# A deeper attention pipeline, with every fourth high half cast on DVE

## The reference

```
x = x + tanh(g_xattn[0]) * xattn(layernorm(x), ctx_2048, ...)     # x, ctx: 8 batches x 256 x 512

q = X @ Wq.T + bq        # 32 heads of 16
k = ctx @ Wk.T + bk      # 8 groups of 16, each group serves 4 heads
v = ctx @ Wv.T + bv
scores = q . k / sqrt(16), masked (a 256 x 256 mask, and a key mask for each batch)
w = softmax(scores)
out = (w @ v) @ Wo.T + bo
```

## Time and profile before

| | us |
|---|---|
| median of 3 runs (1936.1 to 1944.45) | 1940.29 |
| the profiled execution | 1944.32 |
| its span, from the first to the last instruction | 1942.6 |
| busy in the span: PE, PE weight load | 1652.5, 848.3 |
| busy in the span: DVE, ACT, POOL | 975.0, 711.3, 821.8 |

### The profile page before, as it was taken

The page is one execution under the profiler, slowest core; times in us unless marked ns, Lnnn a source line. Parts: engine busy times, 40 slices in busy tenths (PEclk is TensorE's granted clock), DMA queues, the critical chain, the costliest instruction groups (busy, mean ns, idle before and its releaser), DMA issues. The chain is left out here.

```text
span 1942.6 us, 29847 instructions
## 1 busy us (share of the span) xinstructions
PE 1652.5 (85%) x11034; PEld 848.3 (44%) x11034; DVE 975.0 (50%) x1975; ACT 711.3 (37%) x1311; POOL 821.8 (42%) x853
## 2 busy tenths in 40 slices
PE   5589888877874788887799996999999999888897
PEld 3255545544542333433356653444444444343343
DVE  5465556556543577775166563346754333211136
ACT  2176667665674354544122231121111111122221
POOL 1376667666564344444144333423443342011124
PEclk9899999989986899999799997999999999999999
DMA  3531223123141444533346532735654554366655
GB/s 124 144 89 40 72 67 86 41 62 77 29 96 26 85 101 100 98 75 69 66 82 124 103 81 70 159 80 108 125 127 90 124 115 98 76 154 152 153 143 169
DMA packets 423990, 188.36 MB, mean 97 GB/s; under 512 B 365788, under 2 KB 388318, under 8 KB 423848
## 3 DMA queue, kind: packets, MB, share of 16 engines
q1 hardware_dynamic: 418168, 167.85, 38.4%
q0 software_dynamic: 5680, 18.62, 3.8%
HBM read 77.17 MB, written 22.81 MB: 51 GB/s over the span
## 5 line engine op out<-in xcount | busy, mean ns | idle before, releaser
L941 POOL TENSOR_TENSOR a_pl<-a_prob,a_ph 128x512 f16<-128x512 f32 x256 | 294.7, 1162 | 194.3 <-ACT a_prob L862 192.3
L861 ACT ACTIVATE a_ph<-bank 128x512 f16<-128x512 f32 x256 | 153.7, 600 | 148.9 <-PE bank L635 141.2
L1024 DVE TENSOR_REDUCE a_mx<-bank 128x2 f32<-128x512 f32 x256 | 165.4, 684 | 74.8 <-PE bank L617 72.3
L137 PE MATMUL bank<-XTh,d_whs 128*128 128x512 f16 x512 | 195.9, 383 | 0.9 <-ACT e_y L2295 0.7
L138 PE MATMUL bank<-XTl,d_whs 128*128 128x512 f16 x512 | 196.0, 383 | 0.0
L139 PE MATMUL bank<-XTh,d_wls 128*128 128x512 f16 x512 | 195.8, 382 | 0.0
L2133 POOL CAST d_cut<-d_raw 128x512 f16<-128x512 f32 x90 | 57.0, 634 | 239.7 <-DMA d_raw<-in_L_ffn_sw 156.2
L862 ACT ACTIVATE a_prob<-bank 128x512 f32<-128x512 f32 x256 | 154.2, 602 | 0.0
L2053 DVE TENSOR_TENSOR d_hid<-d_hid,bank 128x512 f32<-128x512 f32 x64 | 43.9, 686 | 181.5 <-PE bank L139 181.3
L1266 PE MATMUL bank<-b_wfc,b_xTh 128*128 128x512 f16 x256 | 99.5, 389 | 33.4 <-DMA b_xTl<-f_cut 25.4
L1276 PE MATMUL bank<-b_wpj,b_hTh 128*128 128x512 f16 x256 | 104.7, 409 | 21.9 <-DMA b_hTl<-b_hcut 21.8
(11 more groups left out here) (330 smaller groups left out, 4026.9 us busy)
## 6 DMA issues: line engine op xcount, KB each, us to landing
d_raw<-in_L_ffn_w SPq DMA_DIRECT2D x48, 256.0 KB, 3.1
d_raw<-in_L_ffn_sw SPq DMA_DIRECT2D x42, 256.0 KB, 3.1
made<-e_y SPq DMA_DIRECT2D x39, 256.0 KB, 2.2
a_stage<-in_L_ffn_w_fc SPq DMA_DIRECT2D x32, 256.0 KB, 2.9
a_stage<-in_L_ffn_w_proj SPq DMA_DIRECT2D x32, 256.0 KB, 3.0
a_fbuf<-in_ctx SPq DMA_DIRECT2D x16, 256.0 KB, 3.1
rows<-f_cut SPq DMA_DIRECT2D x16, 256.0 KB, 2.5
out_x<-X SPq DMA_DIRECT2D x16, 256.0 KB, 2.5
```

The costliest lines, as they stand in the source:

```text
L137: nc.tensor.matmul(out_ap, lhi, rhi, start=first, stop=False)
L861: nc.scalar.activation(ph[:, n % NP, :], bank[BST + n % 2][:, :], ACT.Exp)
L941: nc.gpsimd.tensor_tensor(pl[:, n % NP, :], prob[:, n % 2, :], ph[:, n % NP, :], ALU.subtract).then_inc(ev["L"], 1)
L1024: nc.vector.tensor_reduce(mx[:, tt, half, 2 * g:2 * g + 2], bank[BS + m % 2][:, :].rearrange("p (r k) -> p r k", r=2), AX_X, ALU.max)\
```

## The change

Preparation is spread over two batches. In the loop of batch b, q and k, v of batch b+2 are projected (steps 10 to 16) and the first 16 heads of them turned (steps 19 to 22); the other 16 heads of batch b+1 are turned at steps 0 to 3; one plain score and one maximum of batch b+1 stand in every step. The maxima come in halves by heads rather than by queries: those of the first 16 heads leave at step 18, those of the other 16 at step 4 of their own batch, and the turned scores wait for each half only where they begin to use it (steps 0 and 16). `times_v` runs through the end of a batch, the output projection moves to steps 5, 7 and 8, v has three buffers, and the input is loaded one batch earlier. The prologue projects batch 1 as well, inside the plain scores of batch 0, and cuts the input of batch 2.

In steps 2, 6, 10, ... 30 (`CASTS`) ACT takes only the float32 exponential, and DVE makes `ph` by a cast of `prob` from float32 to float16. POOL waits for that cast.

The diff, cut to its core:

```diff
-    vv = sb("a_v", [P, 2, 2, G0, VW], F16)
+    vv = sb("a_v", [P, 3, 2, G0, VW], F16)
...
-    PQ, PK = (0, 3), (1, 4)
-    TQ, TK = (6, 8), (7, 9)
-    FIRST, LAST = 10, 29
+    PQ, PK = (10, 14), (12, 16)
+    TURN0, TURN1 = 19, 0
+    NEG0, NEG1 = 18, 4
+    OTURN, OUT = 5, (7, 8)
+    CASTS = tuple(range(2, 32, 4))
     NORM = LAG + 8
-    OTURN, OUT = 11, (13, 14)
...
-    SUM_AT = [15, 17, 19, 21, 23, 25, 27, 29]
-    CUT_AT = [15, 18, 20, 22, 26, 29]
+    SUM_AT = [1, 5, 9, 13, 17, 21, 25, 29]
+    CUT_AT = [1, 6, 11, 17, 23, 28]
...
@@ PE, turned_scores @@
                 wait("E", b, n + 1, NS)
+                if n % 16 == 0:
+                    wait(f"ng{n // 16}", b, 32, 32)
...
@@ PE, the loop of a batch @@
-                wait("ng", b, 64, 64)
...
-                for n in range(NS + LAG):
-                    if n < NS:
-                        turned_scores(b, par, n)
+                for n in range(NS):
...
+                    turned_scores(b, par, n)
                     if n >= LAG:
-                        times_v(b, par, n - LAG)
+                        times_v(b, n - LAG)
+                    elif b:
+                        times_v(b - 1, NS + n - LAG)
+                    if more:
+                        scores(b + 1, 1 - par, n)
...
                         if n == PQ[tt]:
-                            q_of(nx, tt)
+                            q_of(b + 2, tt)
...
-                    for m in due(n - 1):
-                        scores(nx, 1 - par, m)
...
@@ ACT @@
-                    nc.scalar.activation(ph[:, n % NP, :], bank[BST + n % 2][:, :], ACT.Exp)
+                    if n not in CASTS:
+                        nc.scalar.activation(ph[:, n % NP, :], bank[BST + n % 2][:, :], ACT.Exp)
                     nc.scalar.activation(prob[:, n % 2, :], bank[BST + n % 2][:, :], ACT.Exp).then_inc(ev["E"], 1)
...
@@ POOL @@
                     pool.wait_ge(ev["E"], b * NS + n + 3)
+                    if n in CASTS:
+                        pool.wait_ge(ev["C"], b * len(CASTS) + CASTS.index(n) + 1)
                     nc.gpsimd.tensor_tensor(pl[:, n % NP, :], prob[:, n % 2, :], ph[:, n % NP, :],
                                             ALU.subtract).then_inc(ev["L"], 1)
...
@@ DVE, the loop of a batch @@
                 for n in range(NS):
+                    if n in CASTS:
+                        wait("E", b, n + 3, NS)
+                        nc.vector.tensor_copy(ph[:, n % NP, :], prob[:, n % 2, :]).then_inc(ev["C"], 1)
...
@@ DVE, the prologue @@
             for m in range(NS):
+                if m == 4:
+                    moments(2)
+                if m == 8:
+                    mean(2)
+                if m in (4, 12):
+                    low_q(1, m // 8)
+                if m in (8, 16):
+                    low_kv(1, m // 8 - 1)
+                if m in (21, 25):
+                    take(1, (m - 21) // 4, 0, "q")
+                if m in (23, 27):
+                    take(1, (m - 23) // 4, 0, "k")
                 maxima(0, m)
```

More of the change, by code:

```diff
@@ L519, in _ @@
             place_x(1)
+            load_ctx(2)
             for r in range(KC):
@@ L575, in q_of @@
                     pe.wait_ge(x_tp[b % 2], xt_count(b))
+                    wait("cq", b - 1, 4, 4)
+                if tt == 0 and b >= 2:
+                    wait("nc", b - 2, 2, 2)
+                if tt == 0 and b >= 3:
+                    wait("x0", b - 3)
                 project(bank[BM][:, :], XTh, XTl, wqh, wql, b, tt, f"Q{tt}", "q")
@@ L582, in kv_of @@
                     pe.wait_ge(c_tp[b % 2], ct_count(b))
+                    if b:
+                        wait("ck", b - 1, 4, 4)
+                    if b >= 3:
+                        wait("x1", b - 3)
                 project(bank[BM + 1][:, 0:2 * KV], CTh, CTl, wkvh, wkvl, b, tt, f"KV{tt}", "kv")
[L585 to L604, removed]
+            def turn_q(b, tt, h):
+                if h == 0 and tt == 0:
+                    wait("lq0", b)
+                    wait("lq1", b)
+                    if b:
+                        wait("nc", b - 1, 1, 2)
+                else:
+                    wait("cq", b, 2 * h + tt, 4)
+                for j in range(8):
+                    c = qs[:, tt, 16 * h + 2 * j:16 * h + 2 * j + 2, :].rearrange("p h c -> p (h c)")
+                    last = nc.tensor.transpose(bank16(BM)[:, j * P:(j + 1) * P], c, ident16[:, :])
+                last.then_inc(ev["tq"], 1)
@@ new lines, in turn_k @@
+            def turn_k(b, tt, h):
+                if h == 0 and tt == 0:
+                    wait("lk0", b)
+                    wait("lk1", b)
+                    wait("lv1", b)
+                else:
+                    wait("ck", b, 2 * h + tt, 4)
+                for j in range(8):
+                    c = ks[:, tt, 4 * h + j // 2, 1 - j % 2:3 - j % 2, :].rearrange("p d c -> p (d c)")
+                    last = nc.tensor.transpose(bank16(BM + 1)[:, j * P:(j + 1) * P], c, ident16[:, :])
+                last.then_inc(ev["tk"], 1)
@@ L741, in body @@
                         output(b - 1, OUT.index(n))
-                    if not more:
+                    if more and n == NEG0:
+                        if more2:
+                            wait("lq1", b + 2)
+                        elif b:
+                            wait("x0", b - 1)
+                        turn_maxima(b + 1, 0)
+                    if not more2:
                         continue
@@ L866, in body @@
                         sign(cut_piece(b, n))
-                    if b + 2 < B and n in (11, 13):
-                        normal(b + 2, (n - 11) // 2)
-                    if not more:
+                    if b and n == NEG1:
+                        take_maxima(b, 1)
+                    if b and n == OTURN:
+                        high_output(b - 1)
+                    if more and n == NEG0:
+                        take_maxima(b + 1, 0)
+                    if b + 3 < B and n in (11, 13):
+                        normal(b + 3, (n - 11) // 2)
+                    if not more2:
                         continue
@@ L1114, in body @@
                         residual(b - 1)
[L1115 to L1120 removed]
+                    if b + 3 < B and n == 4:
+                        moments(b + 3)
+                    if b + 3 < B and n == 8:
+                        mean(b + 3)
                     if cut_piece(b, n) is not None:
                         magnitude(cut_piece(b, n))
[L1123 removed]
+                    if more:
+                        maxima(b + 1, n)
+                        if TURN1 <= n < TURN1 + 4:
+                            take(b + 1, (n - TURN1) // 2, 1, "qk"[(n - TURN1) % 2])
+                    if not more2:
                         continue
```

277 lines of the change are left out of this document (148 added, 129 removed).

## The result

The changed kernel takes 1885.1 us (median, 1880.4 to 1887.8), the kernel before, on the same chip, 1942.2. The ratio is 0.971, with an interval of 0.968 to 0.974. The profiled execution took 1885.7 us, 58.6 less than the one of before.

A forecast was written before the change was run, and what follows sets the result against it. No engine was full in phase A, so hand-overs between engines were taken as the bound. 1944 - 58 (batches, casts included) + 10 (prologue) = 1896 us in the profiled execution, 1892 in the median; range 1866 to 1922.

The forecast's parts named there:

- The beginning of a batch: Start of seven batches: the wait of about 4 us for the last maxima and its slow clock go.
- The three stretches: Batch 2 priced as steps 0 to 6, 7 to 17 and 18 to 31: 60.1 us against 64.8.
- The middle stretch: Steps 7 to 17 of batch 2: bound by PE with its products and projections, 26.2 us.
- Steps 0 to 6: First steps of batch 2: bound by DVE, 12.3 us, while PE needs about 10 and waits.
- My third of DVE's small work: In steps 0 to 6 of batch 2: a third of DVE's other 11.8 us assumed there, 3.9 us.
- The ring: Steps 18 to 31: ACT exponentials, POOL subtraction, buffer back to ACT; 14 steps at 1.30 plus small pieces, 21.6 us.
- The prologue: Before the first exponential: batch 1's added work and late transposed x cost 10 us more (5 to 20), 93.5 us.
- 64 casts, about 0.25 each: DVE's casts in all batches: 16 us that the pipeline without them would save; bounds 0 to 1.16 a cast.
- 1 more: Last batch: has casts and nothing else new, so 1 us longer.
- shallower gain: Rival, 1916 us, chance 0.21: casts waiting for ACT delay DVE's maxima and so PE; 3 us more a batch, 24 in all.
- The shared access of DVE and POOL: At each cast: DVE's cast and POOL's instruction lock each other out; by that rule alone the sum is 74 us worse.
- the slower rival: Rival, 1966 us, chance 0.06: each cast locks out POOL, or is locked out, for a full subtraction, 64 x 1.16 = 74.

The follow-up runs named there:

- the late maxima: Changed kernel with the maxima of the next batch's first 16 heads sent off at step 30 in place of 18: 1901.6 us, ratio 0.978.

## Why the prediction was right, and where its sizes were off

The forecast was 1892 us in a range of 1866 to 1922, the measured 1885.1. The mechanisms held; two sizes were off, in opposite directions, so part of the nearness is luck. The pipeline without casts was put at 1892 - 16 = 1876 and measured 1861.6, 14 better; the casts were put at 16 and measured 23.5, 8 worse. The batches alone show less of both: without casts they are 82.8 us less than before, where the forecast had 58 + 16 = 74, and the casts cost 18.9. With casts, batches 0 to 6 were to fall by 59 and fell by 71.2, and the last was to rise by 1 and rose by 7.3.

**The beginning of a batch.** Right, and shown by the late maxima: with a late start of the transfer a wait and a cold clock are back, for 13 to 16 us (21 by the batches). In the changed kernel no wait of 3 us is left there, and batches 1 to 6 run at 0.98 to 1.00. Batch 4 is the exception to the clock of 1.00 at the beginning: behind its wait for the total of the magnitudes the first 6.3 us have 0.80. The other 60 us or so that the batches without casts gain are not divided by any run between the even spread of scores, `times_v` running through, and the moved projections.

**The three stretches.** Batch 2 of the changed kernel, cut at steps 7 and 18:

```profile
204.10:214.40 10.30, 9.07 (x143) 6.61 (x139) 9.20 (x20) 8.76 (x21) 9.45 (x11) 1.00 0.26 86
214.40:241.90 27.50, 27.11 (x272) 15.30 (x272) 13.77 (x27) 16.58 (x39) 16.85 (x16) 1.00 0.32 59
241.90:261.60 19.70, 16.82 (x252) 11.36 (x252) 15.30 (x31) 15.38 (x33) 17.44 (x17) 1.00 0.35 89
```

The middle stretch was to be PE's, 26.2 us without idle time: it is 27.50, with PE busy 27.11. Steps 0 to 6 were to be DVE's 12.3: DVE is busy 9.20 of 10.30. My third of DVE's small work there was an assumption, and too much; PE and POOL are as busy, so no engine alone bounds it. The ring was put at 21.6 and is 19.7. Its plain pace was right (5.1 to 5.2 us for four steps, against 5.2), but the pieces of the next input and the takes, for which I added 3.4 us, are mostly hidden. So batch 2 came to 57.5 in place of 60.1, and batches 1, 3, 4 and 5 were too high in the same way, by 1.3 to 3.4. Batch 0 (53.5, measured 53.0) and batch 6 (50.6, measured 50.5) were right; in batch 6 by luck, because the casts cost 3.6 there, where my price of them was 2.

**The prologue.** 93.5 forecast, 93.2 measured, with PE waiting 7.70 us for the transposed x. The match is closer than the measurement: the kernels with the same prologue have their first `prob` between 90.4 and 93.3. That the transposes bound it is not shown: with x 2.9 us sooner, the first `prob` came later.

**The cast.** The term that was mis-sized is "64 casts, about 0.25 each". They cost 0.37 each by the medians, 0.30 by the batches (18.9 for 64). The cast itself takes 0.43 us in the median and 0.55 on average, about what I took. On the plain ring it costs next to nothing: four ordinary steps take 5.17 us with a cast and 5.13 without. What it costs lies beside the ring, where I had put nothing. In batches 1 to 3 it is step 7 above all, 1.4 us longer: a maximum and the low output, for both of which PE waits, stand behind casts. The largest part, 5.7 of 18.9, comes in the last batch, for which I wrote "1 more". There a scaling for ACT (L1042) stands behind the cast:

```profile
511.68 0.43 DVE L1181 CAST a_ph<-a_prob 128x512 f16<-128x512 f32 x1 [1.60 <-ACT a_prob L904]
512.02 0.25 DVE L1096 RECIPROCAL a_rec<-bank 128x16 f32<-128x16 f32 x1
512.30 0.42 DVE L1099 TENSOR_TENSOR a_on<-bank,a_rec 128x256 f32<-128x256 f32 x1
512.65 2.33 DVE L1042 TENSOR_SCALAR a_stage<-a_stage,b_scale 128x512 f32<-128x512 f32 x2
```

```profile
513.72 0.72 ACT L868 ACTIVATE a_tern<-a_stage,a_unround 128x512 f16<-128x512 f32 x1 [0.74 <-DVE a_stage L1042]
```

DVE stands 1.60 us for `prob`, then does two things of its own, and ACT, whose next exponential is queued behind the sign of that weight piece, stands 0.74 for DVE. A cast makes ACT wait for an engine that was waiting for ACT. In the whole last batch there are five such waits:

```profile
ACT a_tern L868 <- DVE a_stage L1042: 3.9, 5, 0.9
```

Without casts the list of waits of that batch has none. This is the rival "shallower gain" in kind, work that stands in DVE's queue behind a cast that waits for ACT. In its own form, with a maximum behind the cast, it shows once a batch in batches 1 to 3 (1.2 us), and not at each of 8 casts. Its time of 1916 did not come: it laid 24 us on top of the 16 for casts, where all of them cost 19 to 23.5, and on a pipeline that was priced too dear.

**The shared access of DVE and POOL**, by which the slower rival decided, shows in single rows. Where a cast meets POOL's work, it takes 0.65 in place of 0.43, and POOL's piece 1.34:

```profile
247.92 0.65 DVE L1181 CAST a_ph<-a_prob 128x512 f16<-128x512 f32 x1
```

```profile
248.25 1.34 POOL L961 TENSOR_TENSOR a_fcut<-a_fbuf,a_fcut 128x512 f16<-128x512 f32 x1
```

DVE pays for it: 24 of the 64 casts take 0.53 us or more, seven of them 0.99 to 1.30. On POOL's subtractions it does not show: they last 1164 ns with casts and 1165 without (means from 150 to 480 us), where I expected some at 1.3. The subtraction of a cast step waits for its cast anyway. The Trainium skill's page "SBUF — State Buffer", section "Who interferes with whom", has the two lock each other for whole instructions when DVE copies or casts in a two-port mode. Single rows agree, but that each cast waits for a full subtraction does not happen here: 40 of 64 take under 0.5.

**What stays open.** In batches 1 to 3, 1.5 to 1.7 us are lost to casts. Neither leaving out the one at step 6 nor turning the order there brings more than a part back, since the wait of 1.2 us for a maximum stays. It is gone when all casts are issued later, but that edit moves the casts of steps 2 and 6 together. No run takes out the cast of step 2 alone, so its share is argued from the order of the rows. How the losses of batches 4 to 6 divide is open too.

## What to carry to other kernels

An operation that is moved to an engine with spare time is paid for by what stands behind it in that engine's queue while it waits for its input, so look there for work that the first engine needs, not at the busy shares. If the engine that is relieved does not end last, leave the work where it is: here ACT had time for its second exponential, and moving a quarter of them cost 19 us by the batches, 23.5 by the medians. When you price a pipeline in stretches, add small works on top only for the engine that bounds the stretch.

## What the hardware showed that was not expected

A cast from float32 to float16 of 128x512 on DVE takes 0.43 us in the median, less than a scaling of that shape in float32 (0.48 us where nothing meets it). Lifting TensorE's granted clock from 0.64 to 1.00 over a whole batch of 50 us, with extra products, was worth only 1.4 us net. PE was busy 40 of 52 us even at the low clock, so a likely reason is that its products stood beside longer work of ACT and POOL.
